# Cross-attention products of a two-layer decoder as three reduced-precision passes instead of full float32

## The reference, cut to what matters

```python
def _L0_xattn_ref(hidden_states, memory_tokens, memory_mask):
    scores = jnp.einsum('bsd,bmd->bsm', hidden_states, memory_tokens) * scale
    scores = jnp.where(memory_mask[:, None, :], scores, neg_inf)
    attn = jax.nn.softmax(scores, axis=-1)
    readout = jnp.einsum('bsm,bmd->bsd', attn, memory_tokens)
...
    def weight_quant(w):
        scale = 1.0 / jnp.clip(jnp.mean(jnp.abs(w)), EPS)
        return jnp.clip(jnp.round(w * scale), -1.0, 1.0) / scale
```

## Time and profile before

| | us |
|---|---|
| median of 3 runs (lowest, highest) | 1172.32 (1169.99, 1173.95) |
| the profiled execution | 1172.43 |
| its span, first to last instruction | 1170.7 |

### The profile page before, as it was taken

How to read it: one execution, slowest core, us unless ns; L and a number is a source line. 1 busy time by engine, 2 the same in 40 slices (tenths; PEclk the granted TensorE clock), 3 DMA queues, 4 the chain that set the end, 5 groups by cost and what they waited for, 6 DMA issues and landing times.

```text
span 1170.7 us, 15097 instructions
## 1 busy us (share of the span) xinstructions
PE 1055.3 (90%) x5006; PEld 763.2 (65%) x5006; DVE 876.9 (75%) x1644; ACT 583.8 (50%) x1137; POOL 541.9 (46%) x822
## 2 busy tenths in 40 slices
PE   4889999999999999879999779997779999999796
PEld 3768888888888888644545457765656566666443
DVE  5778867886788677724767558866769999999974
ACT  4533343333333333136555447563548777787662
POOL 4465536553655345523778513204544453545420
PEclk9899999999999999989999979998889999999899
DMA  8200000000000000063110025410000121112123
GB/s 299 80 1 1 1 1 2 1 1 1 1 1 1 1 1 5 32 226 120 50 37 1 1 95 198 168 61 1 1 6 17 29 41 36 43 31 48 31 52 87
DMA packets 48428, 52.94 MB, mean 45 GB/s; under 512 B 34528, under 2 KB 35552, under 8 KB 46048
## 3 DMA queue, kind: packets, MB, share of 16 engines
q1 hardware_dynamic: 48352, 51.99, 14.0%
HBM read 39.92 MB, written 4.19 MB: 38 GB/s over the span
## 4 chain that ended last, share of the span: by engine, by line
PE 50%; DVE 18%; POOL 15%; issue 10%; ACT 6%; DMA 1%; DVEq 0%; POOLq 0%; ACTq 0%
PE bank L382 39%; PE bank L458 3%; PE bank L390 3%; POOL pv L2232 2%; ACT b_squares L1637 1%; PE bank L469 1%; POOL wq L2153 1%; POOL wq L2149 1%; DVE at L1311 1%; PE bank L449 1%; DVE o L1341 1%; POOL wq L2142 1%; DVE fm L1424 1%; DVE half_lo L1188 1%; POOL y L2030 1%
## 5 line engine op out<-in xcount | busy, mean ns | idle before, releaser
L382 PE MATMUL bank<-win_hi,a_uT_hi 128*128 128x512 f32 (+1 forms) x320 | 128.2, 401 | 8.7 <-DVE win_lo L819 5.7
L382 PE MATMUL bank<-win_lo,a_uT_hi 128*128 128x512 f32 (+1 forms) x320 | 121.7, 380 | 0.0
L382 PE MATMUL bank<-win_hi,a_uT_lo 128*128 128x512 f32 (+1 forms) x320 | 121.3, 379 | 0.0
L2009 POOL TENSOR_TENSOR da_lo<-upto,dt 128x256 fp32r<-128x256 f32 x128 | 103.6, 838 | 3.4 <-PE bank L382 3.3
L1555 ACT ACTIVATE ex<-bank 128x48 f32<-128x48 f32 x16 | 3.4, 210 | 164.1 <-PE bank L423 164.1
L865 DVE TENSOR_TENSOR da_hi<-upto,dth 128x256 fp32r<-128x256 f32 x128 | 78.9, 664 | 0.0
L382 PEld LDWEIGHTS bank<-win_hi,a_uT_hi 128*128 128x128 f32 x320 | 62.1, 194 | 22.8 <-DVE win_lo L819 6.6
L2030 POOL TENSOR_TENSOR y<-y,off 128x512 f32<-128x512 f32 x24 | 33.7, 1406 | 81.9 <-DVE off L887 81.9
L382 PEld LDWEIGHTS bank<-win_lo,a_uT_hi 128*128 128x128 f32 x320 | 62.0, 194 | 12.6 <-issue 2.9
L382 PEld LDWEIGHTS bank<-win_hi,a_uT_lo 128*128 128x128 f32 x320 | 61.7, 193 | 11.3
L1546 ACT ACTIVATE zs<-bank 128x512 f32<-128x512 f32 x32 | 19.1, 598 | 99.1 <-PE bank L382 99.1
(11 more groups left out here) (317 smaller groups left out, 3055.6 us busy)
## 6 DMA issues: line engine op xcount, KB each, us to landing
wchunk<-w_in SPq DMA_DIRECT2D x32, 256.0 KB, 5.2
stage<-f_in SPq DMA_DIRECT2D x4, 1408.0 KB, 6.3
x<-x_in SPq DMA_DIRECT2D x16, 256.0 KB, 6.6
land<-win_in SPq DMA_DIRECT2D x4, 1024.0 KB, 8.4
wq<-ctxT_in SPq DMA_DIRECT2D x4, 1024.0 KB, 8.5
ctx<-ctx_in SPq DMA_DIRECT2D x4, 1024.0 KB, 5.9
out<-x SPq DMA_DIRECT2D x16, 256.0 KB, 2.7
first_stage<-f_in SPq DMA_DIRECT2D x2, 1408.0 KB, 13.9
```

The lines of the kernel that those rows point to most:

```text
L382: made = e.matmul(bank, a, b, start=start and n == 0, stop=stop and n == len(pairs) - 1)
L2009: made = e.tensor_tensor(da_lo[(2 * G + k) % 4][:], upto[:].unsqueeze(1).broadcast_to([P, HG // 2, P]), dt[m % 2][:, 3, h:h + HG // 2].uns ...
```

## The change

The products `scores` and `recall` are made in three passes of high and low halves, as the feed-forward's are. ScalarE writes the high halves of the turned tile and of the turned weights (in place of its two copies), VectorE the low ones (`low_u`, `low_p`); once per batch ScalarE writes the high halves of keys and values (`high_keys`, `high_ctx`, two pieces of 128x1024 each), and VectorE the low ones (`low_keys`, `low_ctx`). The high and low keys, and the high values, have one buffer each, so those of the next batch wait for the last product of the batch before. The new tiles lie where the first ternary weight was landed; it is now loaded after the last recall, summed in steps 0 to 2 and rounded in steps 3 to 6 of the feed-forward. The order of the calls in the memory stage's loops is new on all four engines, and `recall` of a tile stands one step later.

```diff
             def scores(i):
                 b = i // TPB
                 bank = banks.claim(w, ("scores", i), "masked", i + 1)
-                w.wait_ge("uT_hi", NT + i + 1)
-                w.wait_ge(f"ctxT_loaded_{b}", 16)
-                uT = b_uT[i % 2]
-                product(bank[:], [(uT[:, k * P:(k + 1) * P], wq[:, b, k, :]) for k in range(KD)]).then_inc(
-                    sig("scored"), 1)
+                w.wait_ge("uT_lo", NT + i + 1)
+                for k in range(KD):
+                    w.wait_ge("ctxT_lo", 2 * b + k // 2 + 1)
+                    cols = slice(k * P, (k + 1) * P)
+                    made = product(bank[:], thrice(b_uT_hi[i % 2][:, cols], b_uT_lo[i % 2][:, cols], ctxT_hi[:, k, :],
+                                                   ctxT_lo[:, k, :]), start=k == 0, stop=k == KD - 1)
+                made.then_inc(sig("scored"), 1)
...
+            def low_keys(b, half):
+                rows = slice(half * KD // 2, (half + 1) * KD // 2)
+                w.wait_ge("ctxT_hi", 2 * b + half + 1)
+                e.tensor_tensor(ctxT_lo[:, rows, :], wq[:, b, rows, :], ctxT_hi[:, rows, :].bitcast(F32),
+                                ALU.subtract).then_inc(sig("ctxT_lo"), 1)
...
+            def low_u(i):
+                w.wait_ge("uT_hi", NT + i + 1)
+                e.tensor_tensor(b_uT_lo[i % 2][:], banks.of["u", i][:], b_uT_hi[i % 2][:].bitcast(F32),
+                                ALU.subtract).then_inc(sig("uT_lo"), 1)
...
+            def high_keys(b, half):
+                rows = slice(half * KD // 2, (half + 1) * KD // 2)
+                w.wait_ge(f"ctxT_loaded_{b}", 16)
+                if b:
+                    w.wait_ge("scored", TPB * b)
+                e.activation(ctxT_hi[:, rows, :], wq[:, b, rows, :], ACT.Copy).then_inc(sig("ctxT_hi"), 1)
...
             ffn_up(0)
             for f in range(KF):
-                if f in (0, 6, 13):
-                    ternary_total((0, 6, 13).index(f))
                 if f + 1 < KF:
                     ffn_up(f + 1)
                 ffn_down(f)
+                if f in (2, 6, 12):
+                    ternary_total((2, 6, 12).index(f))
...
                 if f in (4, 6):
                     memory_magic(BATCH - 1, f // 2 - 2)
-                if f in (0, 7, 14):
-                    ternary_scale((0, 7, 14).index(f))
-                for n, first in enumerate((0, 7, 14)):
+                if f in (3, 7, 13):
+                    ternary_scale((3, 7, 13).index(f))
+                for n, first in enumerate((3, 7, 14)):
                     if first <= f < first + QUARTERS:
                         ternary_part(n, f - first)
...
-                for n, first in ((1, 2), (2, 10)):
+                for n, first in ((0, 0), (1, 3), (2, 10)):
                     for part in range(3 * (f - first), min(3 * (f - first) + 3, ABS)):
...
+                if n == 0:
+                    w.wait_ge("recalled", NT)
                 if n == 1:
                     w.wait_ge("route_kept", 3 * BATCH)
+                    w.wait_ge("abs_summed", half * ABS // 2 + 1)
```

More of the change, by code:

```diff
@@ L227, in decoder_kernel @@
         gathered_hi, gathered_lo = (rt.one(n, [P, KD, BATCH * SLOTS], F32R) for n in ("gathered_hi", "gathered_lo"))
+        halves = Region(nc, rt.at, top_end)
+        ctxT_hi, ctxT_lo = (rt.one(n, [P, KD, SEQ], F32R) for n in ("ctxT_hi", "ctxT_lo"))
         place_start = rt.at
@@ L241, in decoder_kernel @@
         rt.at += KD * HID
+        turned = Region(nc, rt.at, rt.at + KD * HID * SIZE[F32])
+        b_uT_hi, b_uT_lo = (turned.ring(n, 2, [P, D], F32R) for n in ("b_uT_hi", "b_uT_lo"))
+        pT_hi, pT_lo = (turned.ring(n, 2, [P, SEQ], F32R) for n in ("pT_hi", "pT_lo"))
+        sc = turned.ring("sc", 3, [P, SEQ])
         first_stage = Region(nc, rt.at, top_end).one("first_stage", [P, KD * HID])
@@ L262, in decoder_kernel @@
         b_squares = ph.one("b_squares", [P, D], BF16)
-        b_u, b_uT = ph.ring("b_u", 2, [P, D]), ph.ring("b_uT", 2, [P, D])
-        sc = ph.ring("sc", 3, [P, SEQ])
-        pT = ph.ring("pT", 2, [P, SEQ])
+        b_u = ph.ring("b_u", 2, [P, D])
         sm = ph.ring("sm", 3, [P, 6])
         u3 = ph.ring("u3", 2, [P, TPB, D])
-        wrow, spare = ph.one("wrow", [P, SEQ]), ph.one("spare", [P, SEQ])
+        wrow = ph.one("wrow", [P, SEQ])
         pick = ph.one("pick", [P, TPB, SLOTS])
+        half_hi, half_lo = ([halves.ring(f"{n}{m}", 2, [P, D], F32R) for m in range(2)] for n in ("half_hi", "half_lo"))
         ph = Region(nc, rt.at, qtmp_start)
         blk_start = ph.at
-        half_hi, half_lo = ([ph.ring(f"{n}{m}", 2, [P, D], F32R) for m in range(2)] for n in ("half_hi", "half_lo"))
         c_h = ph.ring("c_h", 2, [P, BATCH * SLOTS])
@@ L1216, in vector_program @@
                 t0, t1, t2, t3, t4, t5, t6, t7 = (n - lag if 0 <= n - lag < NT else None for lag in range(8))
+                if t2 is not None:
+                    low_ctx(t2, 1)
+                if t0 is not None:
+                    memory_limits(t0)
+                if t1 is not None:
+                    mask_scores(t1)
                 if t5 is not None:
[L1218 removed]
+                    pick_slots(t5)
+                if t0 is not None:
+                    low_ctxT(t0, 0)
@@ L1219, in vector_program @@
                 if t4 is not None:
-                    quantise(t4, 0)
-                if t6 is not None:
-                    quantise(t6, 1)
+                    select(t4)
+                if t0 is not None:
+                    low_u(t0)
+                if t3 is not None:
+                    weigh(t3)
                 if n == NT + 4:
                     low_half(0, 0)
+                    low_half(1, 0)
+                if t1 is not None:
+                    memory_scales(t1)
                 if t2 is not None:
-                    mask_scores(t2)
@@ L1249, in low_h @@
+                if t1 is not None:
+                    low_ctx(t1, 0)
+                    low_p(t1)
+                if t5 is not None:
+                    low_gathered(t5)
+                if t3 is not None:
+                    weights_done(t3)
+                    quantise(t3, 1)
             def low_h(f):
```

206 lines of the change are left out of this document (120 added, 86 removed).

## The result

| | before | changed |
|---|---|---|
| median, us (lowest, highest) | 1171.32 (1169.99, 1173.95), 4 runs | 1185.05 (1182.63, 1187.77), 4 runs |
| span of the profiled execution, us | 1170.7 | 1183.4 |

The changed kernel is slower: ratio 1.0111, 95% interval 1.0085 to 1.0136. The forecast was 1169.5 with a range of 1159 to 1177, so the time lies outside it, on the other side.

The account below looks back on a forecast made before the run. The Tensor Engine was taken as the bound, busy for 90% of the span, with VectorE at 75%. From 1172.43 us, -13.0 in the memory stage and +10.1 in the feed-forward gave 1169.5, range 1159 to 1177.

Parts of the forecast that it names:

- Term 1: Memory stage products: 32 float32 products become twelve fp32r matmuls each, some -0.63 us each, -20.3 us as ceiling.
- Term 2: Memory stage: VectorE gets the low halves, a group takes 37.2 us; together with the shorter products -13.0 us.
- The walk: VectorE's and PE's order followed: 37.2 us per memory-stage group against 40.5; in the feed-forward, PE idle 7.0 us before `ffn_down(5)`.
- rival C: Memory stage: VectorE becomes the bound, groups stay about 40 us, only first eight tiles and tail gain; 1176 us, chance 0.18.
- Term 3: Feed-forward: first ternary weight, moved to steps 3 to 6, meets POOL's quantising and delays `ffn_down(8)`: +10.1 us.
- Rival B: Feed-forward: the ternary operations hardly delay it (0 to +5.5 us); 1163 us, chance 0.18.
- Rival D: Feed-forward: a 7 us idle may drop PE's clock to 1.2 GHz for the products behind; about 1173 us, chance 0.10.

Follow-up runs that it names:

- POOL's operations short: Changed kernel with POOL's eight quantising operations of batches 0 to 2 cut to 128x8: 1160.40 us, ratio 0.9916.
- the kernel with the twelve matmuls more: Changed kernel with twelve matmuls more per batch (batches 0 to 2), result overwritten, while the Tensor Engine waits for the selection: 1183.26 us, ratio 1.0112.
- write-only kernel: Changed kernel with each of POOL's eight quantising operations of batches 0 to 2 replaced by four that only write (iota): 1159.17 us, ratio 0.9888.
- the kernel with recalled values alone: Changed kernel with only recalled values split, scores as one float32 product, batch 3's helper values at the end of feed-forward steps 10 and 12: 1170.49 us, ratio 0.9994.

## Why the prediction was wrong, by its steps

The sums hold but for trifles: the pieces listed for the first tile of a batch add up to 13.25 and not 13.0, and 32 times 0.62 is 19.8 and not 20.3.

- **Term 1** was right in size. Quiet tiles are 6.46 apart (520.39 to 526.85), and PE alone needs 32.0 us for a group, both as worked out. PE was just not the bound.
- **Term 2, VectorE's own work**: right. 31.0 was forecast, 30.3 is what is left without POOL's reading. "It ends up at 31.0 plus whatever waiting is left: 36 to 39" was right as well: 37.6.
- **Term 2, the walk**: here it failed. It took 37.2 us for a group with a busy time of 36 to 39 in it, so with no room for a wait of VectorE, and it was trusted against its own bound. Between the ends of scores 13.0, 6.9, 8.0 and 9.6 were forecast, and 10.9, 6.9, 9.4 and 14.4 came. In the last interval one operation of `select` takes 2.3 us where it takes 0.17 undisturbed, PE idles, and the product behind takes 2.5 more at the lower clock, for which VectorE waits in its turn. The first eight tiles failed in the same way: 5.5 was to be gained up to tile 7, and with POOL's operations short 8.0 more was gained than in the changed kernel (51.8 against 59.8). That memory stage is what rival C describes; it had a chance of 0.18, and its price (1176) was still 9 us too kind, since it let the first eight tiles and the tail gain 6.5. The 1.8 us of the tail (scores of tile 15 to `ffn_up(0)`) didn't come either: its first product took 5.25 us at the lower clock, and in the kernel with the twelve matmuls more, where the clock is up, this stretch is 34.0 and not 36.0.
- **C's "against"**, "POOL's work is unchanged, so each of its operations can block only one", was true and no comfort: the waits in a group stayed at 7.3 us (37.6 less 30.3), but they now lie in the list of the engine that sets the pace, and POOL itself became 4.5 us longer (29.5 to 34.0), where "POOL stays at 29.5" had been forecast. Most of that lies in its small operations, whose `b_mv<-b_sum` of 128x1 has a mean of 0.71 us where it had 0.19.
- **Term 3**: right in place and cause, and in size partly by luck (+10.0 against +10.1). The two waits of PE ended on `hT_lo`, and the ternary operations took 2.98 and 2.94. The first of the three got through at 0.95. The walk has PE idle for 7.0 and 5.8 us; 4.75 and 4.16 came, and the two products behind took 3.9 us more than 2.82 each at the lower clock, a cost that the walk put at nothing. Rival B is out: of the two readings weighed there, that of the Trainium skill ("SBUF — State Buffer", Who interferes with whom), by which a `tensor_scalar` in its two-port mode takes part in the exclusive lock, is the one that the trace bears out (2.98 and 2.94 us for 0.89). The write-only kernel agrees with the same section of the Trainium skill, which says that a VectorE instruction with two SBUF inputs contends with GpSimd instructions that read, not with those that only write: the 128x1 operations went from 0.70 to 0.15 us.
- **Rival D** happened in part, inside the term: the clock was low behind the first wait (0.61 over 727 to 735), the next product took 5.1 us and the one behind the second wait 4.4. VectorE has no gap from one wait to the other, so the first 2.3 us of the slow clock are covered by its backlog; the other 1.6 are on the path (7.2 us from `ffn_down(7)` to `(8)` in place of 5.57).

Left open: why the kernel with recalled values alone, where VectorE is busy for 32.0 and PE for 36.5 of 39.9 us, isn't faster. Its clock (0.94) and POOL's list (31.5) have a part in it; no run separates them.

## What to carry to other kernels

Before moving work from a bound engine to one that is busy for three quarters, take its busy time apart into work and waiting inside instructions; if work plus that waiting comes to the length of the stage, the stage doesn't get shorter, and a walk that says so has left out a wait. Where two engines wait inside their instructions for each other, making one's instructions shorter moved part of the waiting to the other. A one-input operation of 128x1408 beside POOL took three times its length here (2.98 us for 0.89), so where such operations stand relative to POOL's bursts is worth 10 us in one place.

## What the runs showed of the hardware

- An operation on 128x4 took 2.27 us in the group beside POOL's two-input operations, 0.17 with these cut to 128x8 and 0.54 with them write-only.
- POOL pays too: its mean for a 128x256 piece with two full inputs was 0.93 us, four of them 3.7, where one of 128x1024 took 2.35 to 2.52 in the kernel before.
- POOL waits for VectorE as well: the four pieces of one scaling took 2.33 us where VectorE ran no two-input operation beside them, 3.31 where it did.
- POOL's operations that only write (iota, 0.49 us each) left VectorE's 128x1 two-input operations at their undisturbed length (0.15 us).
- The Tensor Engine's clock was at its lower level after it had been busy for 0.87 of 4.5 us, and keeping it up with work that is thrown away was worth no measurable time here.
